# Cross-attention in one batch loop of sixteen steps: one key tile and one value tile per step, maxima from high and low parts, context in quarters

## The reference

```python
x = x + xattn(layernorm(x), ctx, ctx)     # x 16x128x512, ctx 16x2048x512, 16 heads of 32
x = x + attn_block(layernorm(x))          # layer norm, linear attention, GELU MLP
x = x + ffn(layernorm(x))                 # blockwise FP4 linears, SiLU gate

qh, kh, vh = (q @ wq + bq), (k @ wk + bk), (v @ wv + bv)       # in xattn, by head
score = softmax(einsum('bhqd,bhkd->bhqk', qh, kh) / sqrt(32))
out = einsum('bhqk,bhkd->bhqd', score, vh) @ wo + bo
```

## Time and profile before

| | |
|---|---|
| median of 3 runs | 3425.43 us (3423.25 to 3429.36) |
| the profiled execution | 3425.2 us |
| its span, first to last instruction | 3423.4 us |
| mean granted TensorE clock | 0.998 of full speed |
| PE busy | 3384.3 us, 99% |
| DVE, POOL, ACT busy | 2221.6 us (65%), 2081.4 us (61%), 1200.4 us (35%) |
| batches 0 to 14, from the trace | about 141 us each |
| behind batch 15 | about 1077 us, not touched by the change |

### The profile page before, as it was taken

One profiled execution on the slowest core, in us unless ns is written; L12 is line 12 of the kernel. 1 busy time (PEld: TensorE's weight loads), 2 busy tenths in 40 slices (PEclk: granted clock), 3 DMA queues, 4 the chain that ended last, 5 costly groups with the idle time before them and its releaser, 6 DMA issues.

```text
span 3423.4 us, 77272 instructions
## 1 busy us (share of the span) xinstructions
PE 3384.3 (99%) x31304; PEld 2628.8 (77%) x31304; DVE 2221.6 (65%) x3425; ACT 1200.4 (35%) x1655; POOL 2081.4 (61%) x1210
## 2 busy tenths in 40 slices
PE   8999999999999999999999999999999999999999
PEld 6777777777777777777777777777777788878887
DVE  6556556555655655655565565566776688789997
ACT  2244343443434434344344343444223322321111
POOL 3277877878777887778877878762545400023332
PEclk9999999999999999999999999999999999999999
DMA  4111110111101100101011010122222333410000
GB/s 152 50 44 38 38 38 29 47 38 38 38 30 47 50 29 35 50 27 51 29 44 42 26 51 29 48 75 76 72 87 83 128 102 101 130 65 19 25 18 19
DMA packets 83368, 182.96 MB, mean 53 GB/s; under 512 B 7184, under 2 KB 43152, under 8 KB 73872
## 3 DMA queue, kind: packets, MB, share of 16 engines
q1 hardware_dynamic: 83088, 178.63, 15.1%
HBM read 140.59 MB, written 38.01 MB: 52 GB/s over the span
## 4 chain that ended last, share of the span: by engine, by line
PE 92%; DVE 4%; issue 2%; ACT 1%; POOL 1%; DVEq 0%; ACTq 0%; POOLq 0%
PE a_bank L100 67%; PE a_bank L1408 8%; PE a_bank L1453 7%; PE a_bank L1417 6%; DVE x_probsT L1263 1%; PE a_bank L712 1%; PE a_bank L2421 1%; ACT x_probsT L1152 0%; PE a_bank L723 0%; PE a_bank L1472 0%; PE a_bank L1441 0%; PE a_bank L777 0%; PE a_bank L781 0%; DVE s_rden L653 0%; PE a_bank L1426 0%
## 5 line engine op out<-in xcount | busy, mean ns | idle before, releaser
L1251 DVE TENSOR_REDUCE x_maxima<-a_bank 128x1 f32<-128x512 f32 x960 | 608.5, 683 | 741.0 <-PE a_bank L1408 741.0
L949 POOL TENSOR_TENSOR x_pairs<-x_probsT 128x1024 f32<-128x1024 f32 x240 | 571.7, 2382 | 298.2 <-ACT x_probsT L1152 292.9
L100 PE MATMUL a_bank<-x_wv,x_ctx 128*128 128x512 f32 x3072 | 746.0, 396 | 1.1 <-ACT q_out L224 1.1
L100 PE MATMUL a_bank<-x_ctx,x_wk 128*128 128x512 f32 x3072 | 743.3, 396 | 0.0
L1152 ACT ACTIVATE x_probsT<-x_probsT 128x1024 f32<-128x1024 f32 x480 | 507.8, 1058 | 642.1 <-DVE x_probsT L1263 642.1
L100 PEld LDWEIGHTS a_bank<-x_wv,x_ctx 128*128 128x128 f32 x3072 | 563.7, 188 | 167.2 <-DVE x_maxima L1251 27.3
L100 PEld LDWEIGHTS a_bank<-x_ctx,x_wk 128*128 128x128 f32 x3072 | 564.7, 188 | 136.7 <-issue 11.9
L1263 DVE TENSOR_TENSOR x_probsT<-a_bank,x_shift_all 128x1024 f32<-128x1024 f32 x480 | 578.7, 1216 | 138.2 <-ACT x_shift_all L1169 120.1
L1417 PEld LDWEIGHTS a_bank<-x_q,x_k 32*128 32x128 f32 x7680 | 240.8, 186 | 115.5 <-issue 63.0
L1147 ACT ACTIVATE x_v<-a_bank 128x512 f32<-128x512 f32 x256 | 153.1, 598 | 420.6 <-PE a_bank L100 420.6
L1077 POOL TENSOR_TENSOR x_ctx<-x_ctx_raw,x_ctx 128x2048 fp32r<-128x2048 f32 x64 | 293.1, 4579 | 5.0
(11 more groups left out here) (207 smaller groups left out, 3992.8 us busy)
## 6 DMA issues: line engine op xcount, KB each, us to landing
x_ctx_raw<-in_ctx SPq DMA_DIRECT2D x64, 1024.0 KB, 4.8
m_ff_src<-in_w_ff SPq DMA_DIRECT2D x44, 192.0 KB, 2.5
wq_ff<-m_ff_dst SPq DMA_DIRECT2D x44, 192.0 KB, 1.8
attT<-x_out_halves SPq DMA_DIRECT2D x16, 512.0 KB, 2.8
s_attT<-attT SPq DMA_DIRECT2D x16, 512.0 KB, 4.0
m_w_raw<-in_w SPq DMA_DIRECT2D x32, 256.0 KB, 2.9
f_w_in<-wq_ff SPq DMA_DIRECT2D x22, 256.0 KB, 3.5
q_x<-in_x SPq DMA_DIRECT2D x16, 256.0 KB, 4.3
```

The lines of the kernel that those rows point to most:

```text
L100: mm = pe.matmul(out, lhs[a], rhs[b], start=first and n == 0, stop=last and n == 2)
L949: eng.tensor_tensor(pairs[:], probs(i, s)[:, :, 0:2], probs(i, s)[:, :, 2:4], ALU.add).then_inc(paired, 1)
L1251: dve.tensor_reduce(maxima[:, c, g * HG + j:g * HG + j + 1], banks[:, j], AX.X, ALU.max).then_inc(maxed, 1)
```

## The change

- **Order of PE, DVE, ACT and POOL.** `items`, `placed` and the special ends of `macro` go. Each of the 16 steps has one key tile (banks 4 and 5 in turn) and one value tile (bank 0; bank 4 in step 0). `top` for the key tile of step s runs at the start of step s + 1; the sixteenth runs behind step 15. The value tiles of steps 0 to 3 are the last four of batch i itself, the others belong to batch i+1. The loop is cut at step 8 (`front`: steps 0 to 7, `back`: steps 8 to 15), so front(0) and back(14) stand outside it, and four value tiles and the denominators of batch 14 stand ahead of batch 15. `turn` is now in the middle of the key tile of step 0, with `spread` for two groups behind that tile.
- **`top` from high and low parts.** ACT writes each key tile twice (once rounded to float32r in `k_hl[0]`, once in full), DVE makes the low part with one operation that adds the bias, and `top` runs three rounds of 4 float32r matmuls instead of 4 float32 ones. `q_max` is split in the same way once per batch. `first_top`, for batch 0, stays as it was.
- **Context by quarters.** SP loads tiles of 128 rows (256 KB), POOL splits each in two operations of 128x512, one tile per step, each when the value tile of that step is done.
- **End of a batch.** `denominators` of batch i runs in step 1 of batch i+1, the inversion in two halves in steps 1 and 2, POOL's four operations in steps 3 to 6. Some buffers and semaphores are merged; halves are stored one by one.

```diff
-    ITEM_BANKS = (5, 0)
-    ODD_BANKS = (4, 0)
-
-    def items(s):
-
-        if s < DC:
-            return [("k", 0, s)] + ([("v", -1, TPC - 1)] if s == DC - 1 else [])
-        c, half = divmod(s - DC, DC)
-        if half < 2:
-            return [("v", c, 2 * half), ("v", c, 2 * half + 1)]
-        return [("k", c + 1, 2 * half - 4), ("k", c + 1, 2 * half - 3)]
-
-    def placed(s):
-
-        return list(zip(items(s), ODD_BANKS if s > DC and s % 2 else ITEM_BANKS))
+    ALONE = 8
+    WHOLE = NKC + 1
+    SET_UP = 4
+    KEYS_PER = 2
+
+    def key_bank(s):
+
+        return 4 + (s + 1) % 2
+
+    def value_bank(s):
+
+        return 0 if s else 4
+
+    def value_tile(s):
+
+        return divmod((s - DC) % NS, TPC)
...
+        q_max_hl = [sc.at(f"x_q_max{k}", [P, DC, S], F32R, kb) for k, kb in enumerate((103, 95))]
+        k_hl = [sc.at(f"x_k{k}", [P, KC], F32R, kb) for k, kb in enumerate((143, 145))]
...
+        tile_raw = [sc.at(f"x_tile_raw{k}", [P, DC, P], F32, 139 + 2 * k) for k in range(2)]
...
+            def load_tile(i, s):
+                sp.wait_ge(ctx_made, START + tiles_made(i, max(s - 1, 0)))
+                sp.dma_start(tile_raw[s % 2][:], tile_of(i, s)).then_inc(ctx_loaded[s % 2], 16)
...
+            def split_tile(i, s):
+                hi, lo = (a[:, (s // TPC + 1) % 2, :, cols(s % TPC, P)] for a in ctx_t)
+                raw_t = tile_raw[s % 2]
+                pool.wait_ge(ctx_loaded[s % 2], START + (WHOLE * 16 * (1 - s % 2)) + i * (8 * NS) + 16 * (s // 2 + 1))
+                pool.wait_ge(v_done, START + values_done(i, s))
+                pool.tensor_tensor(hi, raw_t[:], one[:].to_broadcast([P, DC, P]), ALU.mult).then_inc(ctx_made, 1)
+                pool.wait_ge(ctx_made, START + tiles_made(i, s) + 1)
+                pool.tensor_tensor(lo, raw_t[:], hi.bitcast(F32), ALU.subtract).then_inc(ctx_made, 1)
...
-            def macro(i, ahead=True):
-                for s in range(NS):
-                    add_up(pool, i, s)
-                    if s in (3, 7, 11):
-                        split_ctx(i + 1, (s + 3) // 4)
-                    if ahead and s == 13:
-                        split_ctx(i + 2, 0)
-                if not ahead:
-                    pool.wait_ge(k_done, START + B * NS)
-                    late.split_output_weights(pool, one)
-                normalise(i)
-                add_bias(i)
...
+            def step(i, s, past=None, ahead=True):
+                if ahead or s < NS - TPC:
+                    split_tile(i, s)
+                add_up(pool, i, s)
+                if past is not None and 3 <= s < 7:
+                    (normalise, add_bias, out_hi, out_lo)[s - 3](past)
...
+            def keys(i, s):
+                c, t = divmod(s, DC)
+                b = key_bank(s)
+                act.wait_ge(k_done, START + i * NS + (NS + s + 1))
+                act.activation(k_hl[0][:], bank[:, b], ACT.Identity, bias=bk_t[:, t:t + 1]).then_inc(k_ready, 1)
+                act.activation(k_t[:, t, cols(c, KC)], bank[:, b], ACT.Identity,
+                               bias=bk_t[:, t:t + 1]).then_inc(k_ready, 1)
+
+            def values(i, s):
+                c, t = value_tile(s)
+                act.wait_ge(v_done, START + values_done(i, s))
+                act.activation(v_t[:, c * TPC + t, :], bank[:, value_bank(s)], ACT.Copy).then_inc(v_ready, 1)
...
+            def query_hi(n):
+                act.wait_ge(q_max_loaded, START + n * 16 + 16)
+                act.activation(q_max_hl[0][:], q_max[:], ACT.Copy).then_inc(q_max_hi, 1)
+
+            def first_step(i, past):
+                query_hi(i + 1)
                 place_rows(i)
-                item(i, "v", NKC - 1, TPC - 2, 5)
                 copy_spread(i, 0)
-                for s in range(NS):
-                    exp(i, s, 0)
-                    for n, (it, b) in enumerate(placed(s)):
-                        if n == 1:
-                            exp(i, s, 1)
-                        item(i + 1, *it, b)
-                    if s < DC - 1:
-                        exp(i, s, 1)
-                        copy_spread(i, s + 1)
-                for v in range(TPC - 2):
-                    item(i + 1, "v", NKC - 1, v, ITEM_BANKS[v])
-                copy_den(i)
+                keys(i, 0)
+                copy_spread(i, 1)
+                exp(i, 0, 0)
+                values(i, 0)
+                if past is not None:
+                    copy_den(past)
+                exp(i, 0, 1)
+
+            def step(i, s):
+                exp(i, s, 0)
+                keys(i, s)
+                if s in (1, 2):
+                    copy_spread(i, s + 1)
+                exp(i, s, 1)
+                values(i, s)
...
+            def key_lo(i, s):
+                t = s % DC
+                dve.wait_ge(k_ready, START + keys_out(i, s))
+                dve.scalar_tensor_tensor(out=k_hl[1][:], in0=bank[:, key_bank(s)], scalar=bk_t[:, t:t + 1],
+                                         in1=k_hl[0][:].bitcast(F32), op0=ALU.add, op1=ALU.subtract).then_inc(k_lo, 1)
...
+            def step(i, s, past=None):
+                if s == 0:
+                    query_lo(i + 1)
+                if s:
+                    maximum_by_head(i + 1, s - 1, tops, (0, 1))
+                add_shift(i, s, 0)
+                if s:
+                    maximum_by_head(i + 1, s - 1, tops, (2, 3))
+                add_shift(i, s, 1)
+                if s and s % 2 == 0:
+                    gather(i, s // 2 - 1)
+                key_lo(i, s)
+                if past is not None and s in (1, 2):
+                    invert(past, s - 1)
...
+            def top(i, m):
+                n, g = i + 1, m % DC
+                pe.wait_ge(maxed, START + HG * n * NS + HG * m)
+                pe.wait_ge(k_ready, START + keys_out(i, m))
+                pe.wait_ge(k_lo, START + i * NS + (m + 1))
+                if m == 0:
+                    pe.wait_ge(q_max_lo, START + n)
+                for k, (a, b) in enumerate(CUTS):
+                    for j in range(HG):
+                        mm = pe.matmul(tops[:, j], q_max_hl[a][rows(j), g], k_hl[b][rows(j)], start=k == 0, stop=k == 2)
                 mm.then_inc(m_done, 1)
...
-            def macro(i):
...
+            def keys(i, s):
+                c, t = divmod(s, DC)
+                if t == 0:
+                    pe.wait_ge(ctx_made, START + tiles_made(i, s))
+                pe.wait_ge(maxed, START + HG * (NS - 1) + i * (HG * NS) + (HG * s + key_bank(s) - HG + 1))
+                item(i + 1, "k", c, t, key_bank(s), (lambda: turn(i)) if s == 0 else None)
+
+            def values(i, s):
+                if s:
+                    pe.wait_ge(shifted, START + i * (2 * NS) + (2 * s + 1))
+                item(i, "v", *value_tile(s), value_bank(s))
+
+            def step(i, s, past=None):
+                if s == 0:
+                    pe.wait_ge(gathered, START + i * TWINS)
+                    pe.wait_ge(shifted, START + i * (2 * NS))
+                    pe.wait_ge(v_ready, START + values_done(i, -1))
+                    score(i, 0)
+                else:
+                    if s == 1:
+                        pe.wait_ge(v_ready, START + values_done(i, 0))
+                        pe.wait_ge(shift_kept, START + shift_at(i, HG + 2))
+                    if s in (2, 3):
+                        pe.wait_ge(shift_kept, START + shift_at(i, HG + s + 1))
+                    if past is not None and s == 1:
+                        pe.wait_ge(shifted, START + i * (2 * NS) + 2)
+                        denominators(past, 3)
+                    pe.wait_ge(gathered, START + i * TWINS + (s - 1) // 2)
+                    top(i, s - 1)
+                    if past is not None and s == 1:
+                        pe.wait_ge(den_out, START + (past + 1))
+                    pe.wait_ge(shifted, START + i * (2 * NS) + 2 * s)
+                    pe.wait_ge(v_ready, START + values_done(i, s - 1))
                     score(i, s)
+                if s and s % 2 == 0:
+                    await_maxed(i + 1, s - 1, 1)
+                    weigh(i, s - 2)
+                    weigh(i, s - 1)
+                keys(i, s)
+                if s < 3:
+                    for g in ((0, 1), (2,), (3,))[s]:
+                        spread(i, g)
+                values(i, s)
+
+            def front(i, past=None):
+                for s in range(ALONE):
+                    step(i, s, past)
+
+            def back(i):
+                for s in range(ALONE, NS):
+                    step(i, s)
                 pe.wait_ge(gathered, START + i * TWINS + (TWINS - 1))
+                top(i, NS - 1)
                 pe.wait_ge(shifted, START + i * (2 * NS) + 2 * NS)
+                weigh(i, NS - 2, b=1)
+                weigh(i, NS - 1, b=1)
...
+            await_maxed(0, NS - 1)
+            front(0)
+            with looped(nc, pe, 0, LAST - 1) as i:
+                back(i)
+                front(i + 1, i)
```

(41 more changed lines are left out.)

359 lines of the change are left out of this document (163 added, 196 removed).

## The result

| | before | after |
|---|---|---|
| median of 15 runs each | 3424.35 us (3422.04 to 3429.36) | 3433.84 us (3429.94 to 3436.74) |
| the profiled execution | 3425.2 us | 3431.2 us |
| its span | 3423.4 us | 3429.3 us |
| mean granted TensorE clock | 0.998 | 0.998 |

The ratio is 1.0027, with an interval of 1.0019 to 1.0035. The change makes the kernel slower by 9.5 us, where I forecast 12.7 us of gain. The other 3.5 us come from where the two profiled executions lie among their runs; what differs between executions of one kernel no trace here shows.

What follows compares the result with a forecast made beforehand. PE, busy 99% of the span, was taken to bound the kernel. Top -21.6, POOL +3.6, batch starts +3.5 and once-only terms +1.8 summed to -12.7, so 3425.2 became 3412.5 us; range 3392 to 3439.

Steps and rivals of the forecast that it cites:

- Only top changes: In the price of a step: tiles, scores and weighs stay, 16 of each kind; 240 tops in batches 1 to 15 change.
- Between batches: End of step 15 to step 4: same work with new waits, 38.1 us for 37.8, 14 times +0.25, +3.5 us.
- A: PE's wait before the next batch's first score, on the last gather: 0.75 us, PE going on at 3.47.
- B: PE's wait in step 1, on ACT's copy of the value tile: 0.75 us, PE going on at 11.97.
- The new top: Each top: 0.75 to 0.80 us for 0.96, value copy binds, gain 0.12 a step, -21.6 us over 12 steps x 15.
- rival 2: In each step: the value tile's copy does not bind, the whole 0.21 to 0.25 is won, 3390 us; chance 0.12.
- Rival 1: In top: the three rounds show their weight loads, top costs 0.99 or more and wins nothing, 3441 us; chance 0.20.
- Rival 3: Batch start longer than counted, for instance by late `q_max`; 1 us more a batch gives 3427 us; chance 0.18.
- the first batch: Batch 0, once: two value tiles move into the steps, and first steps have A's and B's kind of wait, +2.9.
- POOL at step 8: PE's key tile of step 8 waits about 0.26 us for POOL's fourth split, 14 times, +3.6 us.
- Hidden work: 16 new DVE operations and 16 ACT copies a batch are hidden; `key_lo` 0.69 us, quarter split 1.04 + 1.28.

## Why the prediction was wrong

- **The step that failed: the cut at step 8 was not costed.** The prediction says that the tiles, scores and weighs stay, and then "Only top changes". Its sum has no term for PE's jump, though the change puts it directly ahead of a top. Behind each of the 13 jumps the new top is interrupted, 10.5 us in all. That is half of the 21 us between forecast and result.
- **Between batches: right place, wrong size.** This is the second part, +11.5 us for +3.5. A and B exist, with the releasers named, 14 times each. The forecast had 38.1 us (against 37.8 this is 0.3 a batch, of which the sum took 0.25); it is 38.62. PE was to go on at 3.47 and 11.97 us behind the top; it went on at 3.85 and 12.50. The gather and the value copy end close to where I had them (3.51 for 3.42, 12.18 for 11.92). What I had too small is the release: 0.05 us, taken from the step, where it is 0.3 at both places. Why it is longer there was not separated; at both places several waits stand in a row ahead of the work.
- **The new top: right, the size in part by luck.** 1.48 us a batch for the 1.44 forecast, 0.80 us from top to score at the end of 0.75 to 0.80, and the value copy binds. Steps are 7.52 and 9.43 us for the 7.5 and 9.45 forecast. Top and score take 1.86 for 1.85. The gain of 0.12 a step was the smaller of the two that the forecast's own prices give (1.97 and 2.03 less 1.85); it fits because half of the even steps before took 9.53, not the 9.61 of the one that was read. The steps refute rival 2.
- **Rival 1** gave nearly the measured time, for a reason that is not there: its rounds would take 0.99, and they take 0.80. The old top put back costs 17 us more. By the rule of the Trainium skill cited there ("TensorE: Matmul & The Clock Gate", Part 3, the mechanism) the loads of one row group would show in every round; the trace does not agree, with twelve matmuls on the same four groups in 0.80 us. The same section of the Trainium skill also lets a load go ahead into a background weight buffer, and the 0.80 us do not contradict that.
- **Rival 3**, a longer start, is part of what happened (0.5 us a batch over the forecast). Its mechanism, a late `q_max`, struck in batch 0 alone, where the forecast for the first batch was +2.9 and the timeline gives +5.2.
- **POOL at step 8: right in kind, too large.** The forecast was 0.26 us a batch. In the changed kernel there is none: the fourth split ends at 1085.3 and the tile begins at 1086.17, because the pause had made it late by 0.75. With the jump moved and the pause gone, the wait comes out, though the profile books it as "issue": in batches 1 to 13 the key tile follows the end of the split by 0.13 to 0.17 us, 0.13 late with the jump ahead of the tile and 0.07 late with the jump ahead of the score. In batch 0, where POOL has no past result to finish, the split is ready over 1.1 us ahead.
- **Hidden work.** `key_lo` took 0.75 us for the 0.69 of its nearest kind, the quarter split as priced, and in the changed kernel both stayed hidden after batch 0:

```profile
L1121 POOL TENSOR_TENSOR x_ctx<-x_tile_raw,x_one 128x512 fp32r<-128x512 f32 x236 | 245.4, 1040 | 332.4 <-PE a_bank L100 331.2
L1382 DVE SCALAR_TENSOR_TENSOR x_k<-a_bank,x_bk,x_k 128x512 fp32r<-128x512 f32 x240 | 180.1, 750 | 267.5 <-ACT x_k L1214 267.5
L1123 POOL TENSOR_TENSOR x_ctx<-x_tile_raw,x_ctx 128x512 fp32r<-128x512 f32 x236 | 301.1, 1276 | 18.5
```

Still open: why the jump interrupts the new top after eight of its twelve matmuls, and neither a float32 top nor a score nor a key tile. Its length varies from round to round, and leaving the loop can interrupt other work too (a key tile, a weigh). A late supply of instructions would look like this, but the one test of that theory, the score behind the jump, spoke against the form it had here. The runs show what has to stand behind the jump, not the cause.

## What to carry to other kernels

When a change cuts a loop in another place, look at what stands directly behind the jump on the busiest engine, and at what follows when the loop is left; here moving the jump was worth 7.7 us in one place and 10.8 in another. When an engine is busy 99% of the time, list for each new wait what behind it does not need it: two of three repairs only put work that could go first ahead of a wait, some 12 us each. When a large wait goes, look again at the small ones that it hid: POOL's came out only with the pause gone. A gain that is real in every step (22 us here) can be lost at the seams of the loop, and then it pays to mend the seams rather than to undo the change.

## What the hardware showed that I had not expected

- **The jump of the loop.** Twelve float32r matmuls on 32 rows directly behind it are interrupted for 0.24 to 0.79 us, and the step loses 0.50 to 1.07. A float32 top, a score or a key tile behind it lose less than 0.1 us that could be put down to the jump. Leaving the loop interrupted a key tile once for 2.4 to 2.7 us in each of the three kernels that have the jump ahead of one, and a weigh for 1.44 in the one with the old top. For a branch by itself the Trainium skill ("Advanced Engine Details and Errata", Control Flow Timing) gives 0.05 to 0.11 us. Where nothing is interrupted the traces do not contradict it; the losses of 0.50 to 1.07 us it does not explain.
- **DVE beside POOL.** `query_lo` subtracts two operands that both lie in SBUF. Its group, by line (count: duration ns min/median/max):

```profile
L1377 DVE TENSOR_TENSOR x_q_max<-x_q_max,x_q_max x15: 691/1780/1784, 170.4 to 2142.7; 128x512 fp32r<-128x512 f32 x15
```

  It took 0.69 us in batch 0, with POOL idle, and 1.78 (the median) beside POOL's `add_up`, of which one operation took 1.62 us there and 1.30 elsewhere. `key_lo`, as large but with one operand from PSUM, never took over 0.752. The Trainium skill ("SBUF — State Buffer", SBUF: two separate sides) says that a DVE operation with two SBUF inputs and a GpSimd operation that reads SBUF exclude each other on a shared port pair; the trace agrees, by 1.1 us an operation. It cost nothing here, since nothing waits for `query_lo` in that time.
